# Attention's q, k and v projections as three rounded products, with their low parts kept in the idle retention weights

## The reference, cut to what matters

```python
x = x + _L0_attn_a_ref(_layernorm(x), ...)   # retention
x = x + _L0_ffn_ref(_layernorm(x), W_r, W_k, W_v, mu_r, mu_k)
x = x + _L0_attn_b_ref(_layernorm(x), wq, bq, wk, bk, wv, bv, wo, bo, rel_bias)
x = x + _L0_ffn_ref(_layernorm(x), W_r, W_k, W_v, mu_r, mu_k)
...
# in _L0_attn_b_ref
def proj(w, b):
    y = jnp.einsum('blc,dc->bld', x, w) + b
    return y.reshape(Bx, Lx, HEADS, HEAD_DIM).transpose(0, 2, 1, 3)
q, k, v = proj(wq, bq), proj(wk, bk), proj(wv, bv)
scores = jnp.einsum('bhqd,bhkd->bhqk', q, k) / np.sqrt(HEAD_DIM)
attn = jax.nn.softmax(scores + bias[None], axis=-1)
```

## Time and profile before

| | us |
|---|---|
| median of three runs | 2824.11 (2823.85 to 2825.81) |
| the profiled execution | 2824.51 |
| its span in the profile | 2822.7 |
| PE (TensorE matmul) busy | 2696.9 (96%) |
| DVE busy | 2143.4 (76%) |
| ACT busy | 1741.6 (62%) |
| POOL (GpSimd) busy | 1252.9 (44%) |

### The profile page before, as it was taken

How to read it: one execution, slowest core, us unless ns; L and a number is a source line. 1 busy time by engine, 2 the same in 40 slices (tenths; PEclk the granted TensorE clock), 3 DMA queues, 4 the chain that set the end, 5 groups by cost and what they waited for, 6 DMA issues and landing times.

```text
span 2822.7 us, 53686 instructions
## 1 busy us (share of the span) xinstructions
PE 2696.9 (96%) x19682; PEld 1476.0 (52%) x19682; DVE 2143.4 (76%) x4443; ACT 1741.6 (62%) x3671; POOL 1252.9 (44%) x1764
## 2 busy tenths in 40 slices
PE   6989999999999999999999999999999999999998
PEld 5733376433764338643486334854358533575334
DVE  5769856897569966689666996669956799567993
ACT  4428854488544884458744587536874378643885
POOL 3425544255433554335543455434454345433553
PEclk9979999999999999999999999999999999999999
DMA  6150001600015000250002400034000330003300
GB/s 193 31 126 11 24 9 34 146 17 24 9 43 137 17 24 9 57 124 17 31 1 68 113 17 31 1 89 91 17 31 13 97 72 17 31 31 93 59 2 16
DMA packets 71429, 139.18 MB, mean 49 GB/s; under 512 B 12784, under 2 KB 49696, under 8 KB 70016
## 3 DMA queue, kind: packets, MB, share of 16 engines
q1 hardware_dynamic: 69152, 135.29, 19.2%
q10 hardware_dynamic: 2016, 0.45, 0.1%
HBM read 86.02 MB, written 38.82 MB: 44 GB/s over the span
## 4 chain that ended last, share of the span: by engine, by line
PE 70%; DVE 17%; POOL 4%; issue 4%; ACT 2%; SPq 1%; DMA 1%; POOLq 0%; DVEq 0%; ACTq 0%
PE psum L882 18%; PE psum L941 16%; DVE mx L1809 8%; PE psum L655 7%; PE psum L1008 3%; PE psum L659 3%; PE psum L916 3%; PE psum L715 2%; PE psum L1064 2%; PE psum L977 2%; PE psum L842 2%; DVE nrm L1628 2%; POOL X L1926 1%; PE psum L1049 1%; DVE xrT L1639 1%
## 5 line engine op out<-in xcount | busy, mean ns | idle before, releaser
L1809 DVE TENSOR_REDUCE mx<-psum 128x1 f32<-128x512 f32 x2048 | 1265.5, 684 | 81.9 <-PE psum L882 81.1
L1464 ACT ACTIVATE Z<-psum 128x512 f32<-128x512 f32 x2048 | 1110.2, 598 | 273.2 <-PE psum L916 244.6
L2018 POOL TENSOR_TENSOR Z<-Z,W_low 128x256 f32<-128x256 f32 (+1 forms) x1152 | 713.2, 642 | 662.5 <-ACT Z L1464 655.5
L882 PE MATMUL psum<-SK,SQ 63*128 63x512 f32 x2048 | 761.2, 474 | 31.0 <-DVE mx L1809 26.1
L916 PE MATMUL psum<-SQ,SK 64*128 64x512 f32 x2048 | 756.3, 469 | 9.3 <-DMA SQ<-mrow 8.8
L941 PE MATMUL psum<-Z,Vx 128*17 128x256 f32 x8192 | 642.0, 388 | 0.4 <-POOL Z L2018 0.4
L882 PEld LDWEIGHTS psum<-SK,SQ 63*128 63x128 f32 x2048 | 309.0, 190 | 481.3 <-DVE mx L1809 368.0
L916 PEld LDWEIGHTS psum<-SQ,SK 64*128 64x128 f32 x2048 | 309.0, 188 | 81.4 <-ACT Z L1464 37.4
L941 PEld LDWEIGHTS psum<-Z,Vx 128*17 128x17 f32 x8192 | 138.3, 95 | 334.1 <-issue 275.6
L1926 POOL TENSOR_TENSOR X<-X,mixed 128x512 f32<-128x512 f32 x64 | 80.5, 1268 | 274.2 <-DVE mixed L1649 274.2
L1963 POOL TENSOR_TENSOR Z<-Z 128x512 f32<-128x512 f32 x64 | 82.0, 1281 | 244.5 <-DVE Z L1683 244.5
(11 more groups left out here) (135 smaller groups left out, 3535.9 us busy)
## 6 DMA issues: line engine op xcount, KB each, us to landing
W_low<-bias_rows SPq DMA_DIRECT2D x8, 2048.0 KB, 8.8
parts<-Z SPq DMA_DIRECT2D x32, 512.0 KB
W_low<-low_parts SPq DMA_DIRECT2D x7, 1536.0 KB, 6.7
...
```

The source lines that it names most:

```text
L882: pe.matmul(row_bank(c), SQ[rows_of(h, MAX_ROW), h // 2, i * P:i * P + P], SK[rows_of(h, MAX_ROW), h // 2, 512 * k:512 * k + 512], start=T ...
L1464: nc.scalar.activation(ring[:, n % RING, :], col_bank(n), ACT.Exp)\
L1809: nc.vector.tensor_reduce(mx2[:, blk % 2, col, k:k + 1], row_bank(c), AX_X, ALU.max)\
L2018: nc.gpsimd.tensor_tensor(ring[:, n % RING, a:z], ring[:, n % RING, a:z], band_exp[:, 4 * hg + cols_of(s)[i], at:at + z - a], ALU.mult)\
```

## The change

The q, k and v products are made from rounded parts, three products for one. The high parts of the normalised tokens stay in `nT` (written rounded by ACT), those of the weights in `WT`, in place. The low parts of both live in `W_high`, which is idle then: the weights' come from a DRAM copy by a new DMA (`qkv_load`), the tokens' are made by DVE (`ln_lows`: the PSUM value less its rounded copy, two instructions of 128x512 for each 512 tokens). Afterwards the whole of `W_high` is loaded back from DRAM (`high_load`, 2,048 KB), and the next retention waits for that. At the start of the program three instructions make the parts of the weights (`qkv_high`, `qkv_lows`, `qkv_set`) and two more DMAs save them. q and k use three PSUM banks in turn instead of two, so a product waits for the third-last `c_lo` and not the second-last. ACT's waits for the spreading DMAs ahead of the exponentials stand at the first three steps instead of all ahead of them; `mixes(b - 1, 3, (1,))` stands after unit 11 instead of 12; and at the start `constants` stands ahead of the second `rope`, the bias tables in the first step of the loop.

The diff, cut to its core:

```diff
+        wt_at = nc.sbuf_base
         WT = sb("WT", [P, 7, C, D])
+        WT_rounded = nc.alloc_sbuf_tensor_at("WT_rounded", [P, 7, C, D], F32R, offset=wt_at)
...
+        n_parts = (nT_rounded[:, :, 1:1 + T],
+                   W_high[:, QKV_WORDS:QKV_WORDS + C * T].rearrange("p (c n) -> p c n", c=C))
+        qkv_parts = (WT_rounded[:, A_Q:A_V + 1], W_high[:, 0:QKV_WORDS].rearrange("p (w c n) -> p w c n", w=3, c=C))
+        qkv_staged = [SK[:, 4 + 2 * i:6 + 2 * i, :].rearrange("p a n -> p (a n)")[:, 0:QKV_WORDS] for i in range(2)]
...
-        QK_BANK = (3, 7)
+        QK_BANK = (3, 7, 6)
...
             sp.dma_start(low_scratch, W_low_words[:, :]).then_inc(s_saved, 16)
+            sp.dma_start(high_scratch, W_high_words[:, :]).then_inc(s_saved, 16)
+            sp.wait_ge(s_qkv_low, 1)
+            sp.dma_start(qkv_scratch, qkv_staged[1].bitcast(F32)).then_inc(s_saved, 16)
+            sp.wait_ge(s_saved, 48)
+            sp.wait_ge(s_qkv_set, 1)
...
+            def qkv_load(b):
+
+                need(sp, p_g, b, NT)
+                sp.dma_start(W_high_words[:, 0:QKV_WORDS], qkv_scratch).then_inc(qkv_in.sem, 16)
+
+            def high_load(b):
+
+                need(sp, p_qkT, b, 8)
+                need(sp, p_vx, b, 4)
+                sp.dma_start(W_high_words[:, :], high_scratch).then_inc(high_in.sem, 16)
...
+                qkv_load(b)
                 band_load(b)
...
                             spread_rows(b, 2, s)
                         if b > 0:
                             store(b - 1)
+                        if b + 1 < B:
+                            high_load(b)
...
-                    if o == 1 and b < B - 1:
-                        need(pe, c_lo, b + 1, 8)
+                    if b < B - 1:
+                        need(pe, c_lo, b + 1, (6, 8)[o])
...
-                need(pe, c_lo, b, n - 1)
-                for c in range(C):
-                    mm = pe.matmul(bank[QK_BANK[n % 2]], WT[:, A_Q + side, c, h * P:h * P + P],
-                                   nT[:, c, 1 + 512 * g:513 + 512 * g], start=c == 0, stop=c == C - 1)
+                need(pe, c_lo, b, n - 2)
+                if n == 0:
+                    need(pe, qkv_in, b, 1)
+                    if b == 0:
+                        pe.wait_ge(s_qkv_set, 1)
+                for i, j in ((0, 0), (0, 1), (1, 0)):
+                    if i == 1 and n in (0, 2):
+                        need(pe, n_low, b, n + 2)
+                    for c in range(C):
+                        mm = pe.matmul(bank[QK_BANK[n % 3]], qkv_parts[j][:, side, c, h * P:h * P + P],
+                                       n_parts[i][:, c, 512 * g:512 * g + 512],
+                                       start=i + j + c == 0, stop=i == 1 and c == C - 1)
                 mm.then_inc(p_qkT.sem, 1)
 
             def v_project(b, pr):
@@ -848,11 +894,13 @@
                 need(pe, vx_cp, b, pr - 1)
                 if pr >= 2 and b > 0:
                     pe.wait_ge(fn_T, 2 * norm_at(b - 1, 4) + 2)
-                for i in range(2):
-                    t = 2 * pr + i
-                    for c in range(C):
-                        mm = pe.matmul(bank[4 + pr % 2][:, i * D:i * D + D], nT[:, c, 1 + t * P:1 + t * P + P],
-                                       WT[:, A_V, c, :], start=c == 0, stop=c == C - 1)
+                for k in range(2):
+                    t = 2 * pr + k
+                    for i, j in ((0, 0), (0, 1), (1, 0)):
+                        for c in range(C):
+                            mm = pe.matmul(bank[4 + pr % 2][:, k * D:k * D + D], n_parts[i][:, c, t * P:t * P + P],
+                                           qkv_parts[j][:, 2, c, :], start=i + j + c == 0,
+                                           stop=i == 1 and c == C - 1)
                 mm.then_inc(p_vx.sem, 1)
...
                 need(pe, low_in[0], b - 1, 1)
+                need(pe, high_in, b - 1, 1)
...
+            def qkv_high():
+
+                act.wait_ge(s_wts, 7)
+                nc.scalar.copy(qkv_staged[0], WT[:, A_Q:A_V + 1].rearrange("p w c n -> p (w c n)")).then_inc(s_qkv_high, 1)
+
+            def qkv_set():
+
+                act.wait_ge(s_qkv_low, 1)
+                nc.scalar.copy(WT_rounded[:, A_Q:A_V + 1].rearrange("p w c n -> p (w c n)"), qkv_staged[0])\
+                    .then_inc(s_qkv_set, 1)
...
-                    nc.scalar.copy(nT[:, c, 1 + 512 * g:513 + 512 * g], ln_bank(b, n, c)).then_inc(fn_T, 1)
+                    dst = nT_rounded if n in (2, 3) else nT
+                    nc.scalar.copy(dst[:, c, 1 + 512 * g:513 + 512 * g], ln_bank(b, n, c)).then_inc(fn_T, 1)
...
-                for s in range(2):
-                    for pair in range(2):
-                        need(act, spread_pair[pair][s], b, 6)
-                    need(act, first_out[s], b, 2)
-                    need(act, parts_out[s], b, 2)
                 for s in range(NS):
+                    if s == 0:
+                        for pair in range(2):
+                            need(act, spread_pair[pair][1], b, 6)
+                        need(act, first_out[1], b, 2)
+                    elif s == 1:
+                        need(act, parts_out[0], b, 2)
+                    elif s == 2:
+                        need(act, parts_out[1], b, 2)
+                        for pair in range(2):
+                            need(act, spread_pair[pair][0], b, 6)
+                        need(act, first_out[0], b, 2)
...
+            def ln_lows(b, n):
+
+                g = n % 2
+                need(dve, qkv_in, b, 1)
+                need(dve, p_w, b, NT)
+                for c in range(C):
+                    dve.wait_ge(fn_T, 2 * norm_at(b, n) + c + 1)
+                    tok = slice(512 * g, 512 * g + 512)
+                    nc.vector.tensor_tensor(n_parts[1][:, c, tok], ln_bank(b, n, c), n_parts[0][:, c, tok],
+                                            ALU.subtract).then_inc(n_low.sem, 1)
+
+            def qkv_lows():
+
+                dve.wait_ge(s_qkv_high, 1)
+                nc.vector.tensor_tensor(qkv_staged[1], WT[:, A_Q:A_V + 1].rearrange("p w c n -> p (w c n)"),
+                                        qkv_staged[0], ALU.subtract).then_inc(s_qkv_low, 1)
...
             rope(0, 1)
-            constants()
-            bias_tables()
...
+                    if b == 0 and t == 1:
+                        bias_ends()
...
+                        bias_pairs()
...
+                ln_lows(b, 2)
                 ln_norms(b, 3)
...
+                    if n == 2:
+                        ln_lows(b, 3)
...
-                        elif u == 12:
+                        elif u == 11:
                             mixes(b - 1, 3, (1,))
```

30 lines of the change are left out of this document (26 added, 4 removed).

## The result

The changed kernel takes 2875.99 us, the median of four runs (2874.99 to 2877.60), against 2823.98 us before on the same chip: a ratio of 1.0184, 95% interval 1.0166 to 1.0201. The forecast was 2841. The sign was right, the size was not: +52 us instead of +17, outside the range.

What follows compares the result with a forecast made beforehand. TensorE, 96% busy, was taken to bound only some stages, with waits on other engines and SP's queue elsewhere. Products +6, clock +16, row stage -22.4, reload +22.7, start -5.5 gave +16.8 us: 2841, range 2812 to 2864.

Steps and rivals of the forecast that it cites:

- the products' gain doesn't arrive: q, k, v stage: TensorE's 32.3 us saving is lost to waiting for low parts; +0.7 us per sequence, +6 in all.
- Rival (d): TensorE is the bound as the page says and the 32.3 us come out whole: 2787 us; chance 0.08.
- the clock behind the wait for low parts: q, k, v stage: the clock falls to 1.2 GHz in most of eight sequences, 2.0 us each, +16.
- Rival (b): The clock holds after the wait for the low parts, so 16 us go: 2825, no change; chance 0.15.
- the start: Start of the program: TensorE's 5.65 us wait for the mask goes; -5.5 us, bounds -8 and -2.
- the row stage: Mixes one unit earlier: the `xrT` wait shrinks from 2.0 to 0.4 us and its clock fall goes; -22.4 us.
- Rival (c): The row stage gives nothing, through collision with GpSimd or another wait, and the clock falls anyway: 2864 us; chance 0.10.
- The third bank: q, k, v stage: a third PSUM bank for q and k matters little; no size of its own.
- the reload's term: Loop's ninth step: column products wait 4.2 us for maxima behind the load, 1.1 not lost; +22.7 us over seven sequences.
- rival (a): The maxima aren't held up by the reload, so 22.7 us go: 2818.6 us; chance 0.17.
- A fall of the clock in this loop: Long loop: half clock on TensorE costs little, as DVE's pace doesn't depend on it; no term in the sum.
- The slack of 1.0 us: Fourth sequence: second group of maxima put as landing at 1255.2, used at 1256.25; slack nothing in the first sequence.

Runs made afterwards that it cites:

- low_wait_filled: The changed kernel with 19 transposes of the identity ahead of the first product with low parts, in each of the eight sequences: 2854.80 us, ratio 1.0111.
- only_unit_11: The kernel before with `mixes(b - 1, 3, (1,))` after unit 11 instead of 12, nothing else: 2805.44 us, ratio 0.9929.
- reload_filled: The kernel before with the reload and 25 transposes of the identity ahead of the ninth step's first column product, in seven sequences: 2858.18 us, ratio 1.0116.
- unit_11_and_reload: The kernel before with the mixes after unit 11 and with the reload of `W_high` ahead of the second group of maxima: 2852.29 us, ratio 1.0096.

## Why the prediction was right and where it failed

**Right: the products' gain doesn't arrive.** The stage without its clock costs is +4.7 us (forecast +6), and the best version with products is no faster than the best without (2793.92 and 2793.24 us). Rival (d), the page's own 96%, is refuted.

**Right: the clock behind the wait for low parts.** 19 us by low_wait_filled, 16 forecast, and it fell in all eight sequences. Rival (b), that it holds, is refuted.

**Right: the start, and the row stage with luck.** The start gave -6.7 (forecast -5.5). The row stage gave -21.9 (forecast -22.4), but two errors cancel in it. The move alone gives -26.1 (only_unit_11), beyond the bound of -25, and up to -28.9 in low_wait_filled. Against that stand some 7 us of half clock behind the new wait at the first row product, which no term had. Rival (c), that the stage gives nothing, is refuted; the part of it that another wait brings the clock down again came true in four sequences. With unit 11 alone 19 of the 26 us of its stage are left at the end. The third bank brings nothing, as said.

**Wrong: the loop, where the reload's term of +22.7 stood alone and +54.7 was measured.** The mechanism was right: the transfer sits ahead of the maxima in one queue, its bytes decide (half of them, 29.5 us less), and moving it takes 45.4 us away, so rival (a) is refuted. The time of the transfer was right too, 4.8 us against 5.2. The reload's term measured 39.6 us alone and 45.4 to 47.2 beside unit 11, which has 7.5 us of its own in the loop. The sum failed in three steps, and the 32.0 us missing split as follows.

- "DVE sets the pace there and has up to three products left to reduce, so some 1.1 us of that is not lost." Nothing came back. With the reload alone the waits themselves were a little shorter than forecast (24.4 us in sum beyond those of before, where 4.2 each would be 29), yet the steps were 27.8 longer, 3.4 us of it beyond the waits and not explained. The forecast after its credit was 22.7: +5.1.
- "A fall of the clock in this loop costs little, as DVE's pace doesn't depend on it." With the reload alone it costs 1.5 us where it lasts 3.4 us and 2.2 to 2.7 where it lasts 6.8: +11.8, of which filling the wait took 8.9 away. I had priced that very fall at 3.2 us in the row stage and dropped it in the loop, because there DVE is the slower engine at full clock. That holds only at the first steps, where DVE is busy for 6.70 of 6.80 us at half clock. Behind the wait at the ninth step DVE is busy for 3.27 of 6.40 us, and TensorE at 1.2 GHz sets the pace.
- The slack of 1.0 us was an estimate from one sequence of a kernel with the old row stage. In that sequence the store's second half lands at 1256.71, 0.5 us after the column product's start at 1256.25; in the six others with a store it lands 0.3 to 1.5 us ahead of it. So the slack was small from the start. The term for unit 11 and the term for the reload were added, but the one moves the loop towards the backlog of the queue that the other makes longer. Unit 11 alone loses 7.5 in the loop, and together with the reload another 7.6 (54.7 less 39.6 and 7.5): +15.1.

5.1 + 11.8 + 15.1 = 32.0. The range was too narrow for the same reason: its upper end took each cost alone, and the bound of 42 for the reload held waits only. The sizes in the three bullets are differences between runs. The second and the third have experiments of their own (reload_filled, unit_11_and_reload), the first has none.

Not settled: why the steps up to the ninth are 6.0 us longer with unit 11 alone, when the waits for maxima there grew by 2.7 only. With the store moved they get shorter by 3.2 us without products, all of it in these waits, and by 8.9 with products, 5.4 of it outside them. What sets that part wasn't tried.
